# A four-layer graph network on one core: the first layer's coefficients taken as columns of its feature product, the diagonal's low part placed beside high columns

## What is computed

```
# layer 0
h  = relu(layernorm(x)) @ others_weight
u1 = h @ a1 ; u2 = h @ a2
e  = u1[:, idx1] + u2[:, idx2]      # idx: fixed pairs of nodes 2m and 2m+1
e  = where(e >= 0, e, 0.1 * e)
att = softmax(where(adj > 0, e, NEG_BIG), axis=1)
out = att @ h + relu(layernorm(x)) @ self_weight
# layer 1 (graph attention, then a GIN step with an MLP)
h_gat = relu(layernorm((softmax(scores) * A) @ h))
h_gin = (1 + eps) * h_gat + A @ h_gat
z = relu(layernorm(h_gin @ W1 + b1)) ; out = relu(z @ W2 + b2 + h_gat)
# layer 2: graph attention with elu; layer 3: two products, fixed attention
```

## Time and profile before

| | |
|---|---|
| median of 3 runs | 1015.85 us (1012.22 to 1019.29) |
| span of the profiled execution | 1013.8 us |
| PE, DVE busy | 949.6 us (94%), 859.2 us (85%) |
| ACT, POOL busy | 632.5 us (62%), 555.4 us (55%) |
| mean granted TensorE clock | 0.980 of 2.4 GHz |

### The profile page before, as it was taken

One profiled execution on the slowest core, in us unless ns is written; L12 is line 12 of the kernel. 1 busy time (PEld: TensorE's weight loads), 2 busy tenths in 40 slices (PEclk: granted clock), 3 DMA queues, 4 the chain that ended last, 5 costly groups with the idle time before them and its releaser, 6 DMA issues. The chain is left out here.

```text
span 1013.8 us, 21212 instructions
## 1 busy us (share of the span) xinstructions
PE 949.6 (94%) x7355; PEld 902.1 (89%) x7355; DVE 859.2 (85%) x2526; ACT 632.5 (62%) x1655; POOL 555.4 (55%) x1171
## 2 busy tenths in 40 slices
PE   5989999999999999999999999998999999997998
PEld 4779998988998889899989899998999898886897
DVE  5988897989979988977888888799988989779874
ACT  3347547686668653775686664877548584677741
POOL 3535264582575652765566565654636744467850
PEclk9978999999999999999999999999999999999999
DMA  5020000000020010011000101101000100000003
GB/s 135 1 63 1 1 2 1 2 1 1 2 83 2 1 43 2 1 37 49 2 1 2 43 1 43 43 2 33 11 1 2 42 2 2 21 1 2 1 1 105
DMA packets 38071, 19.99 MB, mean 20 GB/s; under 512 B 3142, under 2 KB 37452, under 8 KB 37964
## 3 DMA queue, kind: packets, MB, share of 16 engines
q1 hardware_dynamic: 36080, 18.42, 6.5%
q10 hardware_dynamic: 1884, 0.21, 0.2%
HBM read 10.23 MB, written 8.39 MB: 18 GB/s over the span
## 5 line engine op out<-in xcount | busy, mean ns | idle before, releaser
L686 PE MATMUL ps<-HE,PT 128*128 128x129 f32 x2048 | 238.5, 276 | 3.2 <-issue 1.9
L686 PEld LDWEIGHTS ps<-HE,PT 128*128 128x128 f32 x2048 | 233.1, 192 | 5.4 <-issue 4.8
L451 ACT ACTIVATE Y<-X,SM 128x128 f32<-128x128 f32 x512 | 204.0, 491 | 49.3 <-POOL SM L447 49.1
L1307 DVE SCALAR_TENSOR_TENSOR PT<-ps,CE,maskT 128x512 f32<-128x512 f32 x256 | 174.2, 742 | 19.2 <-PE ps L810 11.8
L432 POOL TENSOR_TENSOR SM<-ST 128x8 f32<-128x8 f32 x96 | 29.5, 307 | 269.4 <-DVE ST L1170 269.3
L443 POOL TENSOR_TENSOR SM<-SM,minus_half 128x8 f32<-128x8 f32 x96 | 163.3, 1701 | 7.6
L686 PE MATMUL ps<-W,HT 128*128 128x128 f32 (+1 forms) x768 | 126.1, 311 | 0.0
L686 PEld LDWEIGHTS ps<-W,HT 128*128 128x128 f32 x768 | 115.6, 193 | 8.9
L1170 DVE BATCH_NORM_STATS2 ST<-X 128x6 f32<-128x128 f32 x512 | 104.8, 278 | 3.1 <-DMA X<-in_x_dram 0.4
L703 PE MATMUL ps<-ident,Y 128*128 128x128 f32 x640 | 85.6, 278 | 10.7 <-ACT Y L451 10.2
L703 PEld LDWEIGHTS ps<-ident,Y 128*128 128x128 f32 x640 | 72.2, 143 | 16.3 <-ACT Y L451 14.4
(11 more groups left out here) (260 smaller groups left out, 2335.6 us busy)
## 6 DMA issues: line engine op xcount, KB each, us to landing
X<-in_x_dram SPq DMA_DIRECT2D x32, 256.0 KB, 3.5
out_dram<-X SPq DMA_DIRECT2D x32, 256.0 KB, 2.8
adj_raw<-in_adj_dram SPq DMA_DIRECT2D x4, 256.0 KB, 3.5
W<-in_L_gnn_W_dram SPq DMA_DIRECT2D x2, 64.0 KB, 3.8
W<-in_L_gnn_W_dram SPq DMA_DIRECT2D x1, 128.0 KB, 3.6
bias<-in_L_gnn_bias_dram SPq DMA_DIRECT2D x2, 64.0 KB, 4.1
Wo<-L_gnn_others_weight_dram ACTq DMA_DIRECT2D x1, 64.0 KB, 3.1
feat1w<-in_L_gnn_Wp_dram ACTq DMA_DIRECT2D x1, 64.0 KB, 3.5
```

The source lines that it names most:

```text
L451: a = nc.scalar.activation(dst[:, n, 0:F], src[:, n, 0:F], func, scale=SM[s][:, S_RSTD, n:n + 1], bias=SM[s][:, S_SHIFT, n:n + 1])
L686: return nc.tensor.matmul(o, w, m, start=start, stop=stop, skip_group_check=True)
L1307: a = V.scalar_tensor_tensor(out=PT[r][:, j, :], in0=o, scalar=CE[s][:, c:c + 1], in1=maskT[:, j, :].bitcast(F32), op0=ALU.max, op1=ALU.mult)
```

## The change

1. **Coefficients as columns.** `feat0w` is the weight `Wo` with two columns more, for u1 and u2 (`WD = 130`). `feat0` now stands right behind `norm0`, has three PSUM tiles (3, 3 and 2 row tiles of 130 columns), and ACT copies them to `HE`. A new step `ucol0` on DVE multiplies the two columns by 1 or 0 for even and odd nodes (`parity`), and splits them into a high and a low part (`UC`). `coef0` on PE is then two fp32r products of the 0/1 matrix `halve` by 32 columns of `UC`, which bring even and odd nodes into the order that is wanted. `coef0` on DVE adds the high and low parts. `wcols0` and its eight products per group are gone. `split0` reads `VA` in SBUF in two whole instructions of 1024 elements.
2. **The diagonal's low part beside high columns.** `gin_mix` has 384 columns per `j`: the low part of the diagonal block and 256 columns of the matrix itself. The second product of a step then covers the 256 columns that are left (for `j` = 0 and 3 two blocks that lie apart).
3. **Own events dropped.** `p_full` is gone: DVE's last `PT` instruction gives the tile back itself, and PE waits for that. In `elu2a`, `elu2b` and `agg3` DVE no longer waits for its own last instruction to send an event (`gated`, `result`); ACT and SP wait for the PSUM tiles' events.
4. `SR` lies in the end of `HT`, `diagv` in `below`.
5. **New order.** `TURNS` and `HOMES` are new.

```diff
     ("norm0", 2, "pe act"),
+    ("feat0", 3, "pe act"),
+    ("ucol0", 0, "dve"),
     ("coef0", 1, "pe dve"),
     ("cmax0", 1, "pe dve act"),
-    ("feat0", 2, "pe"),
...
 TURNS = {
-    "pe": ("gggg0110101020g2120012413240303410101033114040511522553305120232123223032304143130550100001110404151"
+    "pe": ("gggg1010010210g2102012412343000431001340351045121251153035022212312030324334120135003051001104101425"
...
+                link(nc.gpsimd.memset(evens[:], 0.0))
+                link(nc.gpsimd.affine_select(out=stairs[:], in_=work1[:, 0:2, 0:P], compare_op=ALU.is_ge, fill=0.0, base=0,
+                                             pattern=[[P, 2], [-2, P]], channel_multiplier=1))
...
+                pool.wait_ge(made["maskT"], 2)
+                for j in range(T):
+                    lo, c = MIX[j]
+                    nc.gpsimd.tensor_copy(gin_mix[:, j, P - lo * P // 2:3 * P - lo * P // 2], maskT[:, j, c:c + 2 * P].bitcast(F32))
...
@@ PE @@
                 def coef0(u, s):
-                    for b in range(G):
-                        turned(u, "norm0", s, b)
+                    pe.wait_ge(sig["ucols"][s], count(u.g, 1, 0))
                     o, done = open_tile(u, "coef0", s, 0)
-                    for t in range(HALF):
-                        for odd in range(2):
-                            for b in range(G):
-                                c = 4 * ((t * 2 + odd) * G + b)
-                                r0 = t * 2 * P + odd
-                                mm = MM(o[:, c:c + 4], HT[s][:, b, r0:r0 + 2 * P - 1:2], wcols0[:], True, True)
+                    cols = UC[s][:].rearrange("p t c l -> p t (c l)")
+                    for h in range(2):
+                        mm = MM(o[:, 0:4 * TG].rearrange("p (t c) -> p t c", t=HALF), halve[:, h, :], cols[:, h::2, :],
+                                h == 0, h == 1)
...
@@ PE @@
                 def feat0(u, s):
-                    for h in range(2):
-                        o, done = open_tile(u, "feat0", s, h)
-                        for tt in range(2):
-                            for b in range(G):
-                                c = (tt * G + b) * F
-                                mm = MM(o[:, c:c + F], blk(s, b, 2 * h + tt), Wo[:], True, True)
+                    for b in range(G):
+                        turned(u, "norm0", s, b)
+                    for n in range(3):
+                        o, done = open_tile(u, "feat0", s, n)
+                        for c, r in enumerate(range(3 * n, min(3 * n + 3, TG))):
+                            mm = MM(o[:, c * WD:(c + 1) * WD], blk(s, r % G, r // G), feat0w[:], True, True)
...
@@ PE @@
                 def attend(u, name, s, b):
-                    pe.wait_ge(p_full[r], k + 1)
+                    turned(u, "spread" + name[3:], s, 0)
...
@@ PE @@
                 def gin1(u, s):
-                            for m in (LO, HI):
-                                MM(o, m[s][:, j * G + b, :], gin_hi[:, j, :], j == 0 and m is LO, False)
-                            mm = MM(o[:, j * P:(j + 1) * P], HI[s][:, j * G + b, :], gin_lo[:, j, :], False, j == T - 1)
+                            lo, c = MIX[j]
+                            hi = HI[s][:, j * G + b, :]
+                            MM(o, LO[s][:, j * G + b, :], gin_hi[:, j, :], j == 0, False)
+                            MM(whole(o, j), hi, whole(gin_hi[:, j, :], j), False, False)
+                            first = min(c, j * P)
+                            mm = MM(o[:, first:first + 3 * P], hi, gin_mix[:, j, :], False, j == T - 1)
...
@@ ACT @@
+                def feat0(u, s):
+                    rows = HE[s][:].rearrange("p r c -> p (r c)")
+                    for n in range(3):
+                        o, read = filled(u, "feat0", s, n)
+                        first, last = 3 * n * WD, min(3 * n + 3, TG) * WD
+                        A(rows[:, first:last], o[:, 0:last - first], ACT.Copy).then_inc(read, 1)
...
@@ DVE @@
+                def ucol0(u, s):
+                    for n in range(3):
+                        read_by_act(u, "feat0", s, n)
+                    src = HE[s][:, :, F:F + 2].rearrange("p (t b) c -> p t b c", b=G)
+                    both = US[s][:].rearrange("p t (o b c) -> p t o b c", o=2, b=G)
+                    for odd in range(2):
+                        a = V.tensor_scalar(both[:, :, odd], src, parity[:, odd:odd + 1], None, ALU.mult)
+                    link(a)
+                    link(V.tensor_copy(UC[s][:, :, :, 0], US[s][:]))
+                    V.tensor_tensor(UC[s][:, :, :, 1], US[s][:], UC[s][:, :, :, 0].bitcast(F32),
+                                    ALU.subtract).then_inc(sig["ucols"][s], 1)
...
@@ DVE @@
                 def split0(u, s):
-                        a = V.tensor_tensor(YF[s][:, r, :], v, bcast(SM[s][:, S_A, r], F), ALU.mult)
-                        V.tensor_tensor(VA[s][:, r, :], v, bcast(SM[s][:, S_B, r], F), ALU.mult).then_inc(read, 1)
+                    V.tensor_tensor(YF[s], VA[s], bcast(SM[s][:, S_A, :], F), ALU.mult).then_inc(sig["scaled"][s], 1)
+                    V.tensor_tensor(VA[s], VA[s], bcast(SM[s][:, S_B, :], F), ALU.mult).then_inc(sig["scaled"][s], 1)
...
@@ DVE @@
                 def attend(u, name, s, b):
-                    a.then_inc(p_full[r], 1)
-                    dve.wait_ge(p_full[r], u.matrix(name)[1] + 1)
-                    dve.sem_inc(read, 1)
+                    a.then_inc(read, 1)
```

More of the change, by code:

```diff
@@ L126 @@
[L126 to L135, removed]
@@ L201, in gnn_kernel @@
         diag3 = sb("diag3", [P, T])
-        Wo, Ws, W1, W2 = (sb(n, [P, F]) for n in ("Wo", "Ws", "W1", "W2"))
+        Ws, W1, W2 = (sb(n, [P, F]) for n in ("Ws", "W1", "W2"))
         W3 = sb("W3", [P, 2, F])
-        wcols0 = sb("wcols0", [P, 4])
+        feat0w = sb("feat0w", [P, WD])
+        halve = sb("halve", [P, 2, P], F32R)
+        parity = sb("parity", [P, 2])
         feat1w = sb("feat1w", [P, WD])
@@ L276, in matrix @@
                 before = mat_of[m - RING] if m >= RING else None
-                return m % RING, m // RING, before
+                return m % RING, before
         def walk(e, run):
@@ L292, in gnn_kernel @@
         taken = [sem(f"psum_taken{i}") for i in range(BANKS)]
-        p_full = [sem(f"matrix_full{i}") for i in range(RING)]
         sig = {n: [sem(f"{n}_{s}") for s in range(NS)] for n in (
-            "result", "stored", "var", "rstd", "normed", "extent", "scaled", "hi", "lo", "range", "dexp", "by_act",
+            "stored", "ucols", "var", "rstd", "normed", "extent", "scaled", "hi", "lo", "range", "dexp", "by_act",
             "by_pool", "gated")}
@@ L298, in gnn_kernel @@
         x_loaded = [sem(f"x_loaded_{s}") for s in range(NS)]
-        Y, LOW, HE, LOWB, HT, HI, ST, US, CD, CF, CE, CS, MX, SM, DS, HS, SR = ([] for _ in range(17))
+        Y, LOW, HE, LOWB, HT, HI, ST, US, UC, CD, CF, CE, CS, MX, SM, DS, HS = ([] for _ in range(17))
         def slot_first(s):
@@ L384, in gnn_kernel @@
             m_loc = sb("m_loc", [P, MB], F32, sc)
-            diagv = sb("diagv", [P, T, P], F32, sc)
+            diagv = below[:, :, 0:P]
             rmax = sb("rmax", [P, T], F32, sc)
@@ L394, in gnn_kernel @@
         YF = [y[:, :, 0:F] for y in Y]
+        SR = [ht[:, G - 1, N - G * F:N] for ht in HT]
         LO = [low[:, :, 0:F] for low in LOW]
@@ L672, in store @@
                 def store(u, s):
-                    sp.wait_ge(sig["result"][s], count(u.g, 1, 0))
+                    for h in range(2):
+                        slot, k = u.tile("agg3", h)
+                        sp.wait_ge(taken[slot], k + 2)
                     for b in range(G):
@@ L835, in attend, with whole @@
                             mm.then_inc(done, 1)
+                def whole(ap, j):
+                    if j in (0, T - 1):
+                        return ap.rearrange("p (k c) -> p k c", c=P)[:, 0::T - 1, :]
+                    return ap[:, (j - 1) * 2 * P:j * 2 * P]
                 def gin1(u, s):
@@ L1027, in elu2 @@
                 def elu2(u, s):
-                    act.wait_ge(sig["gated"][s], count(u.g, 3, 2))
+                    for name in ("att2a", "att2b"):
+                        for h in range(2):
+                            slot, k = u.tile(name, h)
+                            act.wait_ge(taken[slot], k + 2)
                     A(VA[s], YF[s], ACT.Exp).then_inc(sig["by_act"][s], 1)
@@ L1057, in _ @@
                     "eedge": eedge, "esoft": esoft, "eturn": eturn,
-                    "cmax0": cmax0, "split0": split0, "sums2": sums2,
+                    "feat0": feat0, "cmax0": cmax0, "split0": split0, "sums2": sums2,
                     "scale0": lambda u, s: normalise(u, "norm0", s, Y[s], X[s]),
@@ L1299, in attend @@
                     dve.wait_ge(sig["dexp"][s], count(u.g, 4, 2 * n + 1))
-                    r, k, before = u.matrix(name)
+                    r, before = u.matrix(name)
                     if before is not None:
```

(5 more changed lines are left out.)

108 lines of the change are left out of this document (61 added, 47 removed).

## The result

The changed kernel takes 1041.6 us (median of 4 runs, 1038.1 to 1043.5) against 1014.8 for the kernel before. The ratio is 1.026, 95% interval 1.023 to 1.030: **slower by 2.6%**, where 987 us, faster by 2.8%, was forecast. The profiled run spans 1036.3 us.

What follows compares the result with a forecast made beforehand. TensorE was taken as the bound from 60 us on, VectorE right behind. Coefficients -25.2 and gin1 -7.2, less 3.2 at the start, took 29.2 off the 1013.8 us span; plus 2.05 for the median: 987 us, range 970 to 1003.

Steps and rivals of the forecast that it cites:

- The coefficients: coef0 on TensorE: eight products per group become two short fp32r ones at 0.11 us each, net -25.2 us.
- The diagonal's part: gin1 on TensorE: a step of 512+256+384 columns takes 0.521 us, 0.056 less, over 128 steps -7.2 us.
- TensorE's busy time: Over the whole run, TensorE's busy time should fall to about 918 us with 224 records fewer.
- VectorE: Its occupied time stays or falls by up to 15 us; it has no reason to become the bound.
- ScalarE: Three PSUM copies per group add 22 us, covered by its idle time; busy time about 655 us.
- The start: Coefficients of groups 0 and 1 gain nothing, 3.2 us taken off; the time at 60 us should look the same.
- The longer chain: feat0, ScalarE's copies, ucol0, then coef0: some 2.7 us, with enough TensorE work in between for 12 of 16 groups.
- rival D: Chain through ScalarE and VectorE makes TensorE wait in coef0; decides from 1.8 us per group; 1027 us at 2.5; chance 0.05.
- I let both cancel: Chain waits in uncovered groups, 1 to 2 us each, set against VectorE's freed waits and earlier PSUM banks: net zero.
- Rival E: VectorE and GpSimd block each other as split0 reads SBUF: 6 us on VectorE, 993 us; chance 0.10.
- Rival C: As TensorE gets shorter, its waits for scaled rows grow and take half of 29 us: 1001 us; chance 0.12.
- The sum of 29.2 us: TensorE's total gain: -32.4 us from coefficients and diagonal, less 3.2 us for two groups at the start.

Runs made afterwards that it cites:

- e4: The kernel before with only the diagonal's low part beside high columns, order and banks as before: 1017.9 us, ratio 1.002.
- e7: The changed kernel's whole computation in another order, searched for under the rule that VectorE two-SBUF-input instructions and GpSimd SBUF readers never run together: 985.4 us, ratio 0.971.
- e1: The changed kernel with GpSimd's four 1024-element operations per group replaced by memsets that read no SBUF: 1020.0 us, ratio 1.004.
- e2: The kernel before with GpSimd's four 1024-element operations per group replaced by memsets that read no SBUF: 1010.0 us, ratio 0.997.
- e11: The kernel before with only the attention matrices' own event dropped, order and banks as before: 1010.7 us, ratio 0.995.
- e15: The changed kernel in the old order, GpSimd's reads replaced by memsets (4.1 us chains), first-layer coefficient product given a constant operand: 1020.2 us, ratio 1.004.
- e13: The changed kernel with split0's two SBUF-by-SBUF products replaced by reductions about as long with one SBUF input: 1036.8 us, ratio 1.021.
- e9: The changed kernel with GpSimd's long reads and norm scale-and-shift chains replaced by memsets, chains about 4.1 us: 986.8 us, ratio 0.972.
- e12: The kernel before with GpSimd's long reads and norm scale-and-shift chains replaced by memsets, chains about 4.1 us: 1005.2 us, ratio 0.990.
- e8: The kernel before, computation untouched, in an order searched for in the same way as e7: 1004.3 us, ratio 0.991.
- e5: The changed kernel with GpSimd's long reads and norm scale-and-shift chains replaced by memsets, chains about 3 us: 961.8 us, ratio 0.949.
- e3: The changed kernel's instructions in the order of the kernel before, banks dealt out anew: 1032.8 us, ratio 1.018.

## Why the forecast was wrong, step by step

- **The coefficients** were right: `UC,halve` takes 0.11 us (two from 400.56, the next kind at 400.78), 224 records fewer.
- **The diagonal's part** was right in length (0.52 us a step: 401.39, 401.91, 402.43; its terms add up to 0.524, not to 0.521). That it is worth 7.2 us of time was wrong: alone it brought none (e4).
- **TensorE's busy time** fell to 925.5, not 918. In e7, with the same instructions and fewer waits, it was 909.4.
- **VectorE**: apart from the stretching its busy time is the same in both kernels, as the forecast had it (847.0 us in e1, 847.5 in e2, both nearly unstretched), and the gap behind an attention matrix is gone. That the freed waits are worth nothing was wrong by 5 us (e11). "It has no reason to become the bound" missed the 44.8 us of stretched instructions, 31 more than before.
- **ScalarE** was right: 651.2 us for about 655. The start was nearly right: `emask` ends 1 us later.
- **The longer chain** was right, and rival D falls: the waits for `UC` are 4.6 us in all, 0.3 us a group, where D needed 1.8. Cutting the chain in the old order brought nothing either (e15).
- **The step that failed** is "I let both cancel, so PE's remaining waits stay at what they are". I had counted, from the order, the work that covers the one chain that the change lengthens, and not that of the norm chain, six times a group, though it was the largest wait of the earlier trace rows and the whole order was new. Its waits went from 10.2 to 33.8 us, and all of TensorE's idle time from 64.2 to 110.8.
- **Rival E** had the mechanism, at 6 us; the port's added cost is 45. I counted only `split0`'s 32 instructions (5 us in e13) against GpSimd's four long ones. Left out were the seven long two-input instructions a group that were there before and changed places, the small ones (`CF<-DS,MX`), and the other side: GpSimd's small instructions in the norm chain, held up by VectorE's long ones (e1 to e9: 33 us). "This one alone stands out" misread the trace of before: VectorE has 112 such whole products there, not 64. One is stretched by 1.6 us and two by 0.5, but so are eight of its small instructions, and 55 of GpSimd's by 48.1 us. And it was evidence about the old order only. I should have counted both engines' stretched instructions there, and the meetings in the new order.
- **Rival C** had the right sign (waits for scaled rows grow) and the wrong cause for the loss: not TensorE getting shorter, since without the meetings the change does gain 18 us.
- The sum of 29.2 us for the content: 18.4 (e9, e12) and 18.9 (e7, e8) measured. The missing 10 us go with idle time of TensorE that is 16 us larger in e7 than in e8 (75.9 and 59.9) and in e9 than in e12 (72.4 and 56.9). That it grows because TensorE gets shorter, as rival C had it, fits this and isn't shown by itself.

The account for +26.8 us is thus: content and order without the meetings at the port -18.4, the meetings +45.2, of which 28 at nearly the same stretched time on GpSimd as in the old order. That the new order passes delays of the norm chain on to TensorE is shown (e5 and e9); which of its steps would have to move to stop it is not.

## What to carry to other kernels

A new order of steps is a change of its own: before pricing a change that comes with one, count in it who meets whom, above all VectorE instructions with two SBUF inputs beside GpSimd instructions that read SBUF, in both directions and the small ones too, and how much cover each chain across engines keeps. A short chain of small instructions on GpSimd that feeds the bounding engine is worth more than its busy time: here 1 us in each of 96 such chains was worth 25 us in one order and at most 2 in another. And where a schedule is searched for, let the search know the exclusion: with it the same instructions ran 56 us faster, though how much of that the rule brought isn't separated from the search.

## What the runs showed of the hardware

The exclusion hits tiny instructions at full length: 8 columns on VectorE took 1.47 instead of 0.17 us, 8 columns on GpSimd 1.11 instead of 0.20. It isn't only for two tensors: the pair of L1340, one tensor and a scalar column, was held for 2.1 us as well. There even a GpSimd instruction that only writes is enough, as the pair in e1 shows (0.98 instead of 0.36 us beside a memset), while products of two tensors ran beside memsets at their usual length. The Trainium skill, SBUF — State Buffer, section Who interferes with whom, has `tensor_scalar` among the kinds that can take the shared ports, and the trace agrees.

Waits of TensorE can cost more than themselves. In a wait of 3.47 us that ends at 521.87 the granted clock of the changed kernel falls from 1.00 to 0.50, the level of 1.2 GHz, and stays there to about 538 us, through two shorter waits (0.46 and 1.33 us). Timeline, and windows of PE (busy, records, clock):

```profile
521.87 1.97 PE L728 MATMUL ps<-ident,Y 128*128 128x128 f32 x8 [3.47 <-ACT Y L458]
```

```profile
516.00:520.00 4.00, 2.41 (x20) 1.00 0.00 0
...
524.00:528.00 4.00, 4.00 (x20) 0.50 0.00 0
...
536.00:540.00 4.00, 4.00 (x27) 0.73 0.02 4
```

Eight transposes took 1.97 us there and 1.04 at full clock (492.91). With the same instructions TensorE was busy for 906.7 us in e5, 909.4 in e7, 925.5 in the changed kernel and 930.2 in e3. The clock is a part of that. By their mean granted clocks, 0.972 and 0.978, an estimate is that the changed kernel spent about 58 us of its span at the lower level and e5 about 42; 16 us more at half speed are worth 8 of the 19 us between these two. What the rest is stays open. So a wait of TensorE can be paid for a second time, in a slower stretch behind it; other waits of that length weren't counted for it.
